# Second attention of a two-layer block: the third one-head maximum tile of a step goes behind the next step's first scores, and one output projection starts two steps later

## What is computed

```
q = (x @ q_w.T + q_b).reshape(B, S, H, Dh).transpose(0, 2, 1, 3)
k, v = the same with their weights;  q, k = apply_rope(q), apply_rope(k)
attn = jnp.einsum('bhqd,bhkd->bhqk', q, k) * scaling
probs = jax.nn.softmax(attn, axis=-1)
out = jnp.einsum('bhqk,bhkd->bhqd', probs, v)
out = out.transpose(0, 2, 1, 3).reshape(B, S, D)
return out @ out_w.T + out_b
```

## Time and profile before

| what | us |
|---|---|
| median of 3 runs (lowest to highest) | 801.95 (800.47 to 802.53) |
| the profiled execution | 800.22 |
| its span, first to last instruction | 798.4 |
| second attention with its scores, from the first score matmul to the last steps | 502 to 783 |
| of it with maximum tiles | 502 to 737 |

### The profile page before, as it was taken

How to read it: one execution, slowest core, us unless ns; L and a number is a source line. 1 busy time by engine, 2 the same in 40 slices (tenths; PEclk the granted TensorE clock), 3 DMA queues, 4 the chain that set the end, 5 groups by cost and what they waited for, 6 DMA issues and landing times.

```text
span 798.4 us, 10977 instructions
## 1 busy us (share of the span) xinstructions
PE 723.0 (91%) x4190; PEld 440.3 (55%) x4190; DVE 569.4 (71%) x922; ACT 416.2 (52%) x547; POOL 247.3 (31%) x241
## 2 busy tenths in 40 slices
PE   3678798969698988989999999999999999999997
PEld 3467787957467877656655666433333333333344
DVE  5886766665455665899888998788888278888116
ACT  2532323345253542221122122799999899999983
POOL 0156855333224552231111121012124212412520
PEclk9988999999899999999999999999999999999999
DMA  6145101000101257362211111044434244532411
GB/s 241 54 164 170 49 0 53 1 1 1 53 1 53 80 158 245 104 202 80 83 55 53 54 54 50 20 155 148 140 107 136 84 133 134 162 105 88 127 61 54
DMA packets 25703, 74.13 MB, mean 93 GB/s; under 512 B 4604, under 2 KB 5980, under 8 KB 24692
## 3 DMA queue, kind: packets, MB, share of 16 engines
q1 hardware_dynamic: 21124, 65.37, 24.6%
q0 software_dynamic: 3808, 7.60, 3.3%
q10 hardware_dynamic: 720, 0.48, 0.2%
HBM read 54.54 MB, written 23.06 MB: 97 GB/s over the span
## 4 chain that ended last, share of the span: by engine, by line
PE 66%; DVE 15%; issue 7%; ACT 6%; POOL 3%; DMA 2%; SPq 0%; DVEq 0%; ACTq 0%; POOLq 0%
PE PS L715 20%; PE PS L956 15%; PE PS L942 11%; PE PS L721 9%; PE PS L925 5%; PE PS L915 4%; DVE mx L1235 4%; DMA stg<-in_wa 1%; PE PS L795 1%; DVE XD L1043 1%; ACT P L1409 1%; DVE sg L1174 1%; DVE sg L1166 1%; DVE XL L1050 1%; ACT sg L1375 1%
## 5 line engine op out<-in xcount | busy, mean ns | idle before, releaser
L1409 ACT ACTIVATE P<-PS 128x1024 f32<-128x1024 f32 x256 | 248.8, 1023 | 30.6 <-PE PS L942 29.1
L1242 DVE TENSOR_REDUCE mx<-PS 128x1 f32<-128x512 f32 x288 | 181.4, 684 | 34.3 <-PE PS L925 33.3
L1487 POOL TENSOR_TENSOR hl<-sg,hh 128x512 fp32r<-128x512 f32 x64 | 83.1, 1298 | 219.6 <-ACT hh L1382 219.6
L1235 DVE TENSOR_REDUCE mx<-PS 128x2 f32<-128x1024 f32 x112 | 132.2, 1219 | 15.0 <-PE PS L915 14.8
L942 PE MATMUL PS<-QS,KS 64*128 64x512 f32 x512 | 136.5, 461 | 0.9 <-ACT P L1409 0.7
L956 PE MATMUL PS<-P,VV 128*32 128x512 f32 x1024 | 136.4, 605 | 0.1
L942 PEld LDWEIGHTS PS<-QS,KS 64*128 64x128 f32 x512 | 56.4, 183 | 111.4 <-ACT P L1409 108.5
L1382 ACT ACTIVATE hh<-sg 128x512 fp32r<-128x512 f32 x64 | 40.4, 631 | 135.9 <-DVE sg L1177 84.0
L925 PE MATMUL PS<-KM,QM 64*128 64x512 f32 x288 | 66.3, 415 | 0.0
L1377 ACT ACTIVATE sg<-PS,cols 128x512 f32<-128x512 f32 x32 | 22.0, 688 | 81.6 <-PE PS L715 81.6
L915 PE MATMUL PS<-KM,QM 64*128 64x512 f32 x224 | 51.5, 483 | 9.7 <-DVE mx L1235 7.2
(11 more groups left out here) (199 smaller groups left out, 1348.4 us busy)
## 6 DMA issues: line engine op xcount, KB each, us to landing
QM<-scr_q SPq DMA_DIRECT2D x16, 512.0 KB, 4.5
KM<-scr_k SPq DMA_DIRECT2D x16, 512.0 KB, 5.7
QS<-scr_q SPq DMA_DIRECT2D x16, 512.0 KB, 4.3
KS<-scr_k SPq DMA_DIRECT2D x16, 512.0 KB, 5.2
scr_q<-spl SPq DMA_DIRECT2D x24, 256.0 KB, 3.4
scr_k<-spl SPq DMA_DIRECT2D x24, 256.0 KB, 3.1
scr_o<-OE POOLq DMA_DIRECT2D x14, 256.0 KB, 2.4
stg<-in_tern SPq DMA_DIRECT2D x3, 1024.0 KB, 5.1
```

Of the source, the lines that this page charges most:

```text
L1235: e.tensor_reduce(mx[p % 2][:, :, qt, half], PS[:, b:b + 2, :], AX.X, ALU.max).then_inc(q["mx"], 2)
L1242: e.tensor_reduce(mx[p % 2][:, h, qt, half:half + 1], bank[b], AX.X, ALU.max).then_inc(q["mx"], 1)
L1409: e.activation(P[s % 4][:, half * 1024:(half + 1) * 1024], PS[:, b:b + 2, :].rearrange("p b n -> p (b n)"), ACT.Exp).then_inc(q["ex"], 1)
L1487: e.tensor_tensor(hl[f % 4][:, :], sg[f % 3][:, :], r32(hh[f % 4][:, :]), ALU.subtract).then_inc(q["hl"], 1)
```

## The change

Of the tiles that a step puts, the last is now kept back (`kept`) and put behind `scores(s+1, 0)`. `values(s-1)` follows it. The first projection starts at step 56 instead of 54. Nothing else is edited; the number of tiles, banks and matmuls is the same.

```diff
-PROJECT = (54, 112, 120)
+PROJECT = (56, 112, 120)
...
-    s, loaded = 0, 2
+    s, loaded, kept = 0, 2, 0
...
         if live:
             put("scores", s, 0, st.pair())
+            for _ in range(kept):
+                half_tile(mxr)
...
-            for _ in range(free):
+            kept = min(free, 1)
+            for _ in range(free - kept):
                 half_tile(mxr)
```

## The result

The changed kernel takes 797.73 us (median; 795.89 to 799.50) where the kernel before, beside it, takes 801.95 (799.92 to 804.63). The gain of 4.2 us is over twice the 1.9 that I had forecast.

The account below looks back on a forecast made before the run. TensorE was taken as the bound, its long steps made by waits for VectorE's reductions. -5.0 - 1.2 + 1.3 + 1.9 + 0.2 + 0.9 = -1.9 us, from 801.95 to 800.0; range 797.8 to 802.2.

Parts of the forecast that it names:

- 42 long steps: Steps making maximum tiles beside scores, alternating 2.12 and 2.24 us: the 42 long ones save 0.12 each, -5.0 us.
- projection: At step 54, TensorE's wait for GpSimd's split (OL) goes whole when the projection starts two steps later: -1.2 us.
- output copies: Every eighth step, ScalarE's copy of a pair's sums delays the next scores: 0.15 for nine copies, +1.3 us (0 to 2.7).
- steps with a transpose: Eight steps with a transpose lose a 0.235 us slot each, the scores now standing between tiles a and b: +1.9 us.
- step after the projection: The step following the projections, ScalarE behind and c behind its scores, costs another slot at most: +0.2 us.
- reciprocals: VectorE's 0.24 us reciprocal now stands ahead of c's reduction: 0.11 for eight of them, +0.9 us (0 to 1.9).
- the circle between VectorE's reductions and TensorE's weight loads: Beside scores, c's weights wait 0.29 us for VectorE's reductions; a short step makes the next one long.
- the scores' margin of 0.06: In ordinary steps, first scores' weights can start at 0.41 after ScalarE's exponential; a load at 0.47 still made its slot.
- The rival of hidden handovers: VectorE and ScalarE take reciprocal and copy in idle time of 0.2 to 0.4 us a step: 797.9 us, chance 0.25.
- waited for a DMA: Rival: on VectorE the reciprocal waits for RC's late DMA with c behind it: 804.5 us and more, chance 0.06.
- weights that were not hidden: Rival: c's load behind scores on the same half takes 0.10 us in every step: 810.7 us, chance 0.02.
- the 802.4 of its costs: The forecast time with both handovers, output copies and reciprocals, at their upper ends: +0.5 us, 802.4.

Follow-up runs that it names:

- run 6: The kernel before, with one-head reductions reading 256 of each tile's 512 columns (maxima of half the columns): 795.72 us, ratio 0.9917.
- run 1: The changed kernel with the first projection left at step 54, so the moved tile alone: 797.6 us, ratio 0.9948.
- Run 2: The kernel before with only the first projection moved, from step 54 to 56: 801.61 us, ratio 1.0002.
- run 3: The changed kernel, but in steps with a transpose both tiles stay ahead of the next scores: 797.64 us, ratio 0.9957.
- run 5: The changed kernel with one-head tiles reordered, head 0 of two tiles, then head 1 of the same two: 799.97 us, ratio 0.9976.
- run 8: The changed kernel with two more small reciprocals behind each reciprocal, ahead of the kept tile's reduction: 800.89 us in a single run.
- run 4: The changed kernel with the reciprocals of fourteen of sixteen pairs put back behind the kept tile's reduction: 797.67 us, ratio 0.9945.
- run 7: The changed kernel with a second copy of the same sums into a scratch tile on ScalarE: 806.09 us in a single run.

## Why the prediction was wrong

The forecast's terms, against the steps of the two profiled executions (us; a step's length less 2.12, summed over the steps of a kind):

| term | forecast | measured |
|---|---|---|
| 42 long steps | -5.0 | -5.1 |
| projection | -1.2 | -0.86 at its first step; -0.75 with the transpose that moved into it; -0.55 with the foldings that it moved |
| output copies | +1.3 | +1.3 |
| steps with a transpose | +1.9 | +0.2 |
| step after the projection | +0.2 | +0.14 |
| reciprocals | +0.9 | +0.06 |
| second attention | -1.9 | -3.96 |

The mechanism, the circle between VectorE's reductions and TensorE's weight loads, was right, and so was its size (run 6 shows the cause, runs 1 and 2 that the moved tile brings all of the gain). The 2.1 us by which the sum is off are errors that partly cancel: two costs were counted too high, by 2.5 together, and one gain by 0.65.

**The step that failed is the transposes' +1.9.** I counted three slots because I took the matmuls to begin in the order of the program, so that the second head's scores could not pass the first head's, which wait for tile a's half. I gave this term one value and no ends. And the trace of before already held the passing, in every ordinary step after step 0 whose third tile lies on the first head's half. In the long step of the earlier trace rows it is this row of score matmuls, which begins beside c:

```profile
542.33 0.71 PE L942 MATMUL PS<-QS,KS 64*128 64x512 f32 x2
```

The record at 542.33 carries the update of the scores' semaphore, so it is the second head's; the first head's begins at 542.66. I read such a slot as c beside "one head's scores" and did not ask which head's. In the changed kernel the steps with a transpose stayed at 2.29 to 2.31 (rows above, run 3), the second head's scores passed the first head's, and run 5 shows the rule that holds here: slots are counted on the fuller half. With it the seven steps have two slots, as before, and the sum is -3.5; only step 1, where the scores come late from ScalarE, paid its 0.23.

**The reciprocals' +0.9** was a size. The ends, 0 and 1.9, held what came. I took 0.11 of the 0.24, but a reciprocal pushes VectorE back by 0.16 only, and the load that follows comes at 0.68 into the step instead of 0.59 (523.54), just inside its margin (at 0.92, in run 8, it costs 0.23). What was paid is 0.06 in step 23, where a pair's folding falls ahead of the reciprocal, a meeting that I had not looked for; run 4 moves the reciprocal and finds no gain. Steps 85, 95 and 96 lost 0.20 more, where the pairs now end at another tile. That belongs to the moved projection: run 1, without it, has none of it.

**The projection's -1.2** was too large. I let the wait for OL go whole without asking what stood under it, the bank of the same step's first tile. And I said that eight steps without tiles remain eight, but one of them now holds a transpose: it is 2.62 instead of 2.31, of which the step that the transpose left gives back 0.20. Third, from there on the pairs' foldings fall ahead of a tile's reduction, another 0.20. Run 2 measures the move alone as nothing, and the changed kernel's second attention is 0.10 longer than run 1's. The wait itself hangs on DMAs (run 1).

**What was right.** Copies leave their mark on eight steps, 0.14 to 0.16 each, as worked out from the scores' margin of 0.06, and run 7 shows that a second copy is not hidden either, though there most of it is the values' wait for the bank. The rival of hidden handovers (797.9) came nearest to the time, but by its reason it holds for the reciprocals alone: the copies were not hidden, and most of the difference lies in the transposes, which it did not speak of. No reciprocal beside maximum tiles waited for a DMA, and no ordinary step showed weights that were not hidden.

The range was too narrow by the transposes' missing lower end: with 0 there, the lower bound would have been 795.9. Two figures of the forecast don't follow from its own sums: the upper end of the range, 802.2, lies below the 802.4 of its costs, and weights that are not hidden give 808.8, not 810.7 (801.95 - 1.9 + 8.7). Neither bears on what failed.

## What to carry to other kernels

Where two kinds of matmuls use different parts of the rows, count the slots of each part, and don't add a slot for their order before a row shows it. A term for an order of work needs two ends until a row shows that order, even where its arithmetic looks plain; look first whether the trace holds it in another place. Before a wait is taken out whole, look for the next wait in the same instruction's dependences: the bank that it writes as much as the data that it reads.

## What the runs showed of the hardware

- Matmuls on the two halves of the rows advance by themselves: behind a transpose, a tile, both scores and another tile take two slots in a step of 2.29 (533.71 to 536.00), although their order in the program would take three if none could pass another; the second head's scores begin 0.33 ahead of the first head's (534.34 and 534.67), and so they do in the kernel before beside a third tile (542.33 and 542.66); with three of the four on one half it is 2.52 (run 5). The Trainium skill ("TensorE: Matmul & The Clock Gate", section "The mechanism") says that matmuls start and end strictly in program order; these steps do not agree with it.
- On VectorE a 0.24 us reciprocal between two reductions moves the second by 0.16 (537.97 to 538.13); two more move it by 0.22 together (537.63 to 537.85). On ScalarE a copy of 0.60 was followed by the next instruction after 0.48 (524.87, 525.35, 525.83).
- In all runs the part of the kernel ahead of the second attention, which no edit touched, differed by up to 3.9 us between profiled executions (501.79 to 505.7). From 200 to 300 us the mean granted clock of TensorE was 0.97 of full speed before and 0.93 in the changed kernel, which fits the later start; in the second attention, from 505 to 780 us, it was 1.00 in both. One profiled execution's total can't show a gain of 4 us here; the stage's own length can.
